# An LSTM step with its scan for h split in two: one for the first digit, one for both

## What is computed

```
def step(carry, xs):
    h, c = carry
    i_t = sigmoid(xi_t + h @ V_i)
    f_t = sigmoid(xf_t + h @ V_f)
    g_t = tanh(xg_t + h @ V_c)
    o_t = sigmoid(xo_t + h @ V_o)
    c_new = h * c + i_t * g_t
    h_new = o_t * tanh(c_new)
    return ((h_new, c_new), h_new)
```

## Time and profile before

| what | before |
|---|---|
| median of three runs | 4465.63 us |
| profiled execution | 4453.07 us, its span 4451.1 us |
| PE busy | 3811.0 us (86%) |
| DVE busy | 3318.3 us (75%) |
| ACT busy | 2653.9 us (60%) |
| POOL busy | 2153.8 us (48%) |
| mean granted TensorE clock | 0.525 |
| steps with the LSTM | 3136 |

### The profile page before, as it was taken

One profiled execution on the slowest core, in us unless ns is written; L12 is line 12 of the kernel. 1 busy time (PEld: TensorE's weight loads), 2 busy tenths in 40 slices (PEclk: granted clock), 3 DMA queues, 4 the chain that ended last, 5 costly groups with the idle time before them and its releaser, 6 DMA issues.

```text
span 4451.1 us, 131885 instructions
## 1 busy us (share of the span) xinstructions
PE 3811.0 (86%) x35548; PEld 2512.2 (56%) x35548; DVE 3318.3 (75%) x18750; ACT 2653.9 (60%) x11804; POOL 2153.8 (48%) x2998
## 2 busy tenths in 40 slices
PE   3678888888888888888888888989888888888887
PEld 2455555555555555555555555555555555555554
DVE  3337777777787878777878787777777777777776
ACT  1336666666666666666666666666666666665555
POOL 6665454545454545454545454545454545452222
PEclk9775555555555555555555555555555555555555
DMA  4000000000000000000000000000000000000000
GB/s 66 1 1 1 1 1 1 1 1 1 1 1 1 1 1 1 1 1 1 1 1 1 1 1 1 1 1 1 1 1 1 1 1 1 1 2 1 1 1 1
DMA packets 44542, 11.08 MB, mean 2 GB/s; under 512 B 39913, under 2 KB 44010, under 8 KB 44490
## 3 DMA queue, kind: packets, MB, share of 16 engines
q1 hardware_dynamic: 42378, 10.05, 1.4%
q10 hardware_dynamic: 2112, 0.46, 0.1%
HBM read 7.29 MB, written 3.21 MB: 2 GB/s over the span
## 4 chain that ended last, share of the span: by engine, by line
PE 47%; DVE 22%; ACT 18%; issue 8%; POOL 4%; DVEq 0%; POOLq 0%; SPq 0%; DMA 0%; ACTq 0%
PE GATES L1037 20%; ACT O L561 10%; DVE H L719 10%; DVE O L712 9%; ACT G L558 8%; PE YB L888 6%; PE DB L984 4%; PE YB L991 4%; PE TAPB L875 4%; PE DB L869 3%; POOL HD L396 2%; PE H1B L903 1%; PE H2B L903 1%; PE GATES L1017 1%; POOL ACC L407 1%
## 5 line engine op out<-in xcount | busy, mean ns | idle before, releaser
L558 ACT ACTIVATE G<-GATES 128x12 f32<-128x12 f32 x3136 | 565.0, 180 | 1385.1 <-PE GATES L1037 1321.7
L1037 PEld LDWEIGHTS GATES<-H,VN 128*128 128x128 f16 x9408 | 511.8, 109 | 1426.1 <-DVE H L719 1413.3
L1037 PE MATMUL GATES<-H,VN 128*128 128x4 f16 x9408 | 761.4, 175 | 494.2 <-DVE H L719 439.4
L707 DVE TENSOR_TENSOR_SCAN CT<-G,CT 128x16 f32<-128x16 f32 x3136 | 613.1, 196 | 523.8 <-ACT G L558 394.2
L396 POOL TENSOR_TENSOR HD<-VV,DBS 128x448 f32<-128x448 f32 x480 | 541.9, 1129 | 470.0 <-ACT DBS L550 317.9
L561 ACT ACTIVATE O<-G 128x8 f32<-128x8 f32 x3136 | 662.0, 211 | 99.3
L719 DVE TENSOR_TENSOR_SCAN H<-O,CT 128x20 f16<-128x20 f32 x3136 | 614.1, 196 | 122.4
L1037 PE MATMUL GATES<-H,VW 128*128 128x4 f16 x9408 | 696.0, 168 | 0.0
L712 DVE RECIPROCAL O<-O 128x4 f32<-128x4 f32 x3136 | 566.7, 181 | 142.7
L389 POOL TENSOR_TENSOR PA<-PA,XN 128x336 f32<-128x336 f32 x392 | 328.1, 837 | 630.3 <-ACT PA L515 630.1
L888 PE MATMUL YB<-HD,W 128*64 128x112 f32 x3840 | 606.7, 416 | 25.6 <-POOL HD L396 19.9
(11 more groups left out here) (202 smaller groups left out, 5383.4 us busy)
## 6 DMA issues: line engine op xcount, KB each, us to landing
out_dram<-OUT SPq DMA_DIRECT2D x112, 28.0 KB, 2.0
X<-in_x_dram SPq DMA_DIRECT2D x4, 672.0 KB, 12.1
STG<-in_L_ffn_w_dram SPq DMA_DIRECT2D x4, 512.0 KB, 7.1
U<-in_L_conv_U2s_dram SPq DMA_DIRECT2D x1, 972.0 KB
W<-in_L_ffn_w_dram SPq DMA_DIRECT2D x1, 512.0 KB, 9.1
X<-in_x_dram ACTq DMA_DIRECT2D x4, 112.0 KB, 3.2
S<-in_L_conv_S1s_dram SPq DMA_DIRECT2D x1, 108.0 KB
S<-in_L_conv_S2s_dram SPq DMA_DIRECT2D x1, 108.0 KB
```

The costliest lines, as they stand in the source:

```text
L558: act.activation(G4[:, :, 1:4], gates[c][:, w, :, :], ACT.Tanh, scale=1 / GSCALE).then_inc(step_in, 1)
L707: dve.tensor_tensor_scan(CELL.rearrange("z b k -> z (b k)"), G4[:, :, :].rearrange("z b k -> z (b k)"), ADD4.rearrange("z b k -> z (b k)") ...
L1037: last = pe.matmul(gates[c][:, w, :, SLOT[g]], wt[:, g].rearrange("z m c -> z (m c)"), H5[:, :, d], start=False, stop=True, skip_group_che ...
```

## The change

A second tile HR holds the result of a scan of its own, O5 gets two copies, and PE takes its first three products from HR after `hd1_done`, the last three from H5 after `hd2_done`. Copy 0 of O5 has a zero in place 3 (never written), so that its scan needs no reciprocal. The semaphore `hd_in` is replaced by `t_done` and `rec_done`. The o copy of ACT writes both copies of O5.

```
-        O5 = sb("O5", [128, B, 5])
+        O5 = sb("O5", [128, 2, B, 5])
+        HR = sb("HR", [128, B, 5], F16)
...
-                    act.activation(O5[:, :, 1:5:3], G4[:, :, 3:4].broadcast_to([128, B, 2]), ACT.Copy, scale=O_MAX, bias=1.0)\
+                    act.activation(O5[:, :, :, 1:5:3], G4[:, :, 3:4].unsqueeze(1).broadcast_to([128, 2, B, 2]), ACT.Copy, scale=O_MAX, bias=1.0)\
                         .then_inc(o1_done, 1)
                     act.wait_ge(cell_done, 1 + n + 1)
                     act.activation(TC5[:, :, 0:4:3], CELL[:, :, 2:3].broadcast_to([128, B, 2]), ACT.Tanh, scale=0.5)\
-                        .then_inc(hd_in, 1)
+                        .then_inc(t_done, 1)
...
                     dve.wait_ge(o1_done, 1 + n + 1)
-                    dve.reciprocal(O5[:, :, 3], O5[:, :, 1]).then_inc(hd_in, 1)
+                    dve.reciprocal(O5[:, 1, :, 3], O5[:, 1, :, 1]).then_inc(rec_done, 1)
                     if t == HALF - 2:
                         dve.wait_ge(ocopy_done, 1 + 4 * (j - LAG))
                     if t == W - 3:
                         dve.wait_ge(ocopy_done, 1 + 4 * (j - LAG) + 2)
 
-                    dve.wait_ge(hd_in, 1 + 2 * n + 2)
-                    dve.tensor_tensor_scan(H5[:, :, :].rearrange("z b k -> z (b k)"), O5[:, :, :].rearrange("z b k -> z (b k)"),
+                    dve.wait_ge(t_done, 1 + n + 1)
+                    dve.tensor_tensor_scan(HR[:, :, :].rearrange("z b k -> z (b k)"), O5[:, 0].rearrange("z b k -> z (b k)"),
+                                           TC5.rearrange("z b k -> z (b k)"), 0.0, op0=ALU.mult, op1=ALU.add)\
+                        .then_inc(hd1_done, 1)
+                    dve.wait_ge(rec_done, 1 + n + 1)
+                    dve.tensor_tensor_scan(H5[:, :, :].rearrange("z b k -> z (b k)"), O5[:, 1].rearrange("z b k -> z (b k)"),
                                            TC5.rearrange("z b k -> z (b k)"), 0.0, op0=ALU.mult, op1=ALU.add)\
                         .then_inc(hd2_done, 1)
-                    dve.tensor_tensor(HIST[:, t, :], O5[:, :, 1], TC5[:, :, 0], ALU.mult).then_inc(h_done, 1)
+                    dve.tensor_tensor(HIST[:, t, :], O5[:, 0, :, 1], TC5[:, :, 0], ALU.mult).then_inc(h_done, 1)
...
-                    pe.wait_ge(hd2_done, 1 + n)
-                    for wt, d in ((VN, 2), (VW, 4)):
+                    for done, wt, digit in ((hd1_done, VN, HR[:, :, 2]), (hd2_done, VW, H5[:, :, 4])):
+                        pe.wait_ge(done, 1 + n)
                         for g in range(3):
-                            last = pe.matmul(gates[c][:, w, :, SLOT[g]], wt[:, g].rearrange("z m c -> z (m c)"), H5[:, :, d],
+                            last = pe.matmul(gates[c][:, w, :, SLOT[g]], wt[:, g].rearrange("z m c -> z (m c)"), digit,
                                              start=False, stop=True, skip_group_check=True)
```

More of the change, by code:

```diff
@@ L231, in build_program @@
         (dupx_done, xh4_done, xl4_done, pre0_done, pre1_done, gates_done, step_in, o1_done, cell_done,
-         hd_in, hd2_done, h_done, ocopy_done, oadd_done, ostored) = lstm_sems = sems(
+         t_done, rec_done, hd1_done, hd2_done, h_done, ocopy_done, oadd_done, ostored) = lstm_sems = sems(
             "dupx_done xh4_done xl4_done pre0_done pre1_done gates_done step_in o1_done cell_done "
-            "hd_in hd2_done h_done ocopy_done oadd_done ostored")
+            "t_done rec_done hd1_done hd2_done h_done ocopy_done oadd_done ostored")
         counted = norm_sems + inv_sems + gate_sems + expert_sems + row_sems + lstm_sems
@@ L771, in _ @@
             link(dve.tensor_copy(MLO[96:128, :], ID[96:128, 97:98]))
-            for tile_, v in ((DP, 0.0), (XS, 0.0), (HIST, 0.0), (G4, 0.0), (O5, 0.0), (H5, 0.0), (WC, 0.0), (IDUP, 0.0), (BX, 0.0), (ONEH, 1.0)):
+            for tile_, v in ((DP, 0.0), (XS, 0.0), (HIST, 0.0), (G4, 0.0), (O5, 0.0), (HR, 0.0), (H5, 0.0), (WC, 0.0), (IDUP, 0.0), (BX, 0.0), (ONEH, 1.0)):
                 link(dve.memset(tile_[:], v))
-            link(dve.memset(O5[:, :, 2:3], -1.0))
+            link(dve.memset(O5[:, :, :, 2:3], -1.0))
             link(dve.tensor_copy(IOT[:, :], IOTI[:, :]))
```

## The result

The changed kernel takes 4422.84 us (median of four runs, 4422.48 to 4425.43), the kernel before 4465.64 (four runs, 4461.49 to 4466.09): ratio 0.9905, 95% interval 0.9891 to 0.992. It is faster by 43 us, where 22 us slower was forecast. The profiled executions lie closer together: 4422.99 and 4453.07 us, spans 4421.2 and 4451.1, 30 us apart.

What follows compares the result with a forecast made beforehand. The prediction took the LSTM step, a 1.28 us ring run 3136 times, as the bound. Plain steps -0.16 and late steps +0.55 net +0.39 us a row, +22 us over 56 rows; ratio 1.005, likeliest 4488 us, range 4463 to 4512.

Steps and rivals of the forecast that it cites:

- -0.035 + 0.11 - 0.08 is nothing within the rounding: TensorE's six recurrent products: earlier first loads and later last loads cancel; gain taken as 4 ns, bounds -10 to +10.
- plain step: One of 40 LSTM steps of a row's 56 without a late term; together forecast at -0.16 us a row.
- a plain step shorter than 1.27: Stated sign that the forecast is wrong; the step was expected within 0.01 of 1.28 us.
- third rival: DVE's lateness is covered and early products pay, through an earlier second scan or closer loads; 4447 to 4456 us, chance 0.09.
- first rival: On DVE the first scan can't start before the reciprocal has ended; +100 us on top, about 4590 us, chance 0.05.
- second rival: On DVE the second scan waits for the end of the first; 4730 to 4850 us, chance 0.05.
- late steps: Steps 0, 5, 8, 12, 18, 48, 51 and 53, where DVE's lateness of 0.075 isn't covered; +0.55 us a row.
- Steps 18 and 51: TensorE held up by DVE's late gate addition, or through POOL's last product by DVE's late VV; +0.075 us each.
- 12 and 53: Steps where fillers L629 and L632 on DVE hold back the cell scan; +0.02 and +0.085 us.
- The fillers PD and VV: DVE filler products after L724, forecast to fit before the next cell scan, PD by 0.035 us.
- The o copy of 16 elements: ACT writes 16 elements for 8 on the reciprocal's path, which has slack; bounds 0 to 10 ns, taken as 0.
- nothing changes: Steps where TensorE's own filler ends late, so the first three products start when it is done; 8 of 56, no change.

Runs made afterwards that it cites:

- second_waits: The changed kernel with the second scan made to wait for the end of the first; 5084.14 us, ratio 1.1405 to the kernel before.
- scan_behind: The kernel before with one more scan of 20 elements, its result unused, behind the scan for h; 4490.81 us, ratio 1.007.
- regs_ahead: The changed kernel with TensorE working out step 10's two filler wait values before waiting for the first scan; 4415.01 us, ratio 0.9884 to the kernel before.
- before_regs: The kernel before with TensorE's two filler wait values of step 10 worked out ahead of the products; 4461.63 us, ratio 0.9997.
- three_places: The changed kernel with the first scan over 12 elements for 20, strided tiles, o copy writing 8 elements; 4413.45 us, ratio 0.988 to the kernel before.

## Why the prediction was wrong

**The step that failed: "-0.035 + 0.11 - 0.08 is nothing within the rounding"**, the price of the products. The second scan was priced at its lone duration of 196 ns, with a start 0.11 behind the first. The start was right. But it ends 171 ns after its start, so it frees the last three products 25 ns sooner than reckoned: -0.035 + 0.11 + 0.171 - 0.196 - 0.08 = -0.03. In place of a gain of 4 ns (bounds -10 to +10) a plain step gains 0.02 to 0.03. 40 steps x 0.022 x 56 = 49 us more gain; the forecast of +22 becomes -27, and the profiled executions differ by -30. The second_waits run shows that nothing else changed in that instruction: with nothing running in front, it takes 196 ns again. The prediction had named this sign of being wrong itself, a plain step shorter than 1.27.

Could the rows have told? HIST starts behind a running scan in every step of the kernel before, and there is none of it alone to compare, so the row gave a start but no end. Elsewhere that trace has both signs. MAX8 (L677) is 178 ns long alone and 160 in the 62 cases where it starts some 95 ns behind the start of another MAX8 (the two at 1825.30 and 1825.40, for example); the reciprocal, 108 ns behind a cell scan, keeps its 181. So a shorter second scan was not certain, but it belonged in the bounds. They were taken on the start alone (0.11 to 0.23), with the duration as fixed. 14 ns of it were enough to turn the sign, as the third rival's own threshold says.

**What was right.**
- The first scan doesn't wait for the reciprocal: 0.64 behind the gate tanh for 0.67. The first rival (0.05) is out, DVE starts it when the tanh's semaphore arrives: in plain steps at 636 ns behind the gate tanh (median), 32 behind the end of the cell's tanh and 10 before the end of the reciprocal.
- The second scan starts 0.11 behind it. The second rival (0.05) is out. The trace of the change shows it in every step: the second scan starts 111 ns or more behind the first, 112 in the median, and the first is 196 long.
- The late steps. Eight were named; their sum was forecast at +0.55 us a row and is +0.05 + 0.09 + 0.01 - 0.03 + 0.08 + 0.07 + 0.08 + 0.04 = +0.39. Steps 18 and 51, which hang on DVE's lateness through TensorE and POOL, cost what was said. Those that pass through the scans are some 0.02 cheaper each, 12 and 53 0.05. Some 0.02 is the same mis-sized term (the product L728 starts 0.05 later behind the gate tanh than L724 did, for 0.075); the rest of 12 and 53 wasn't traced. scan_behind confirms the sum by itself (+33 us for +26), with step 15 in it, which was on no list.
- The fillers PD and VV do not push the cell scan, although only 0.035 was left for PD. The shorter second scan helps here too: L728 starts 0.36 behind HR (1992.31 to 1992.67), where 0.39 was reckoned.
- The o copy of 16 elements takes 220 ns for 211, and the reciprocal ends 10 ns later; both are off the path.

**What was missing.** Step 10: "nothing changes" in the steps where TensorE's own filler ends late. It costs +0.06 to 0.07 a row, about 4 us. The first of the filler's register operations, 65 ns ahead of the last three loads before, now starts 2 ns behind their start. The loss goes when the wait values are worked out ahead of the products (regs_ahead), and the same lines bring less where the products have one wait (before_regs).

**The third rival** (the early products pay, 0.09) had the right sign and the right threshold: a plain step must save 14 ns to decide. Its mechanism was not the one at work. It put the gain on a start under 0.10 or on closer loads; the start stayed at 0.11, the last three loads and their products are no closer (0.079 from the first of the three loads to the start of the last product, before and after), and the gain came from the end of the scan. The sign of this rival came true by another way than its own.

Worked by row: 40 plain steps x -0.026 = -1.04, eight late ones +0.39, step 10 +0.07, together -0.58; x 56 = -32 us. The LSTM starts 2.5 us later (325.7 for 323.2), which leaves -30, the difference of the spans. The means over all rows give the same: -1.03, +0.38 and +0.07 us a row.

**Open:** the 13 us between the difference of the medians and that of the profiles. It belongs to the kernel before, whose mean step is 1.3150 in one execution and 1.3171 in another. The difference of these two lies in the plain steps, where TensorE's last product starts 3 ns later in the one; that is 6.6 us, and the executions of 4466 us weren't profiled. What makes an execution take the one or the other wasn't found.

## What to carry to other kernels

An instruction that starts behind a running one is to be priced from end to end, not by its start plus its lone duration: here the second scan adds 0.11 + 0.171 - 0.196 = 0.085, and not 0.11. When a result is split so that a consumer can start on its first half, the gain is what no longer stands behind the second half (three loads, 0.08), less what the second half adds (0.085), plus what the first half no longer waits for (0.035); then walk through every step of the filler schedule for work that the extra instruction makes late, since that took back nearly half of the gain (0.46 of 1.04 us a row). The wait in the middle of TensorE's products also held up the register operations of the filler that came next: in step 10 the first starts 89 ns behind the start of the first loads, for 13 before.

## What the runs showed of the hardware

- A scan of 20 elements that starts 0.11 behind the start of a running scan of 20 is 169 to 171 ns long in the records, and 196 alone (the change, scan_behind, second_waits). Behind a scan of 12 elements it is 179. HIST is 133 ns long behind a running scan, and 159 in the 52 cases of second_waits in which nothing runs when it starts.
- An overlap of 10 ns with the reciprocal didn't shorten HR: it is 196 ns long in the 2754 of 3136 steps in which it starts before the reciprocal ends (by 10 ns in the median of all steps), and 196 in the others.
- The scan of 12 elements is 178 ns long, the one of 20 196; the scan behind them starts 0.096 and 0.112 us after their start (medians of three_places and the change).
- Where one more wait stood in front of a scan on DVE, it was a semaphore instruction of its own in the trace, and the scan started 0.065 to 0.07 us behind its start (second_waits; steps 26 and 53 of the kernel before).
- Step 10, register operations of TensorE's filler (medians over the rows): the first starts 13 ns behind the start of the first loads in the kernel before, where one wait stands in front of the products, and 89 ns behind it in the change, 2 ns behind the start of the loads that follow the second wait. L873 starts 0.194 behind the start of the last three loads in the change and 0.079 in regs_ahead.
- The first load of the filler starts 0.026 us behind the last recurrent load at the least where both tiles are 128*128, and 0.120 at the least where the filler's is 128*64, 112*32 or 33*128 (the change; L886 and L862, L892, L1004 and L857).
- TensorE's granted clock is 0.52 to 0.53 of full speed as a mean of the span in all runs (0.521 in second_waits, 0.526 in regs_ahead), and 0.50 from 333 us to the end, before and after alike. In the PEclk row of the page the first three slices are 9, 7, 7 before and 9, 7, 6 after, and all others 5.
